# The last finish of a four-layer graph network: cosine multiply on GpSimd, statistics by tile, store in five parts

## The reference

```python
def _layernorm(x, axis=-1, eps=1e-05):
    m = jnp.mean(x, axis=axis, keepdims=True)
    v = jnp.var(x, axis=axis, keepdims=True)
    return (x - m) / jnp.sqrt(v + eps)
...
# the end of the last layer (L3)
    angle = 0.1 * (ms @ W3) * node_attr * (1.0 / np.sqrt(MUL0 + MUL1))
    cos, sin = (jnp.cos(angle), jnp.sin(angle))
    return cos * sc + sin * conv
...
x = _layernorm(x + _L0_gnn_ref(x, ...), axis=-1)
...
x = _layernorm(x + _L3_gnn_ref(x, ...), axis=-1)
```

## Time and profile before

| | us |
|---|---|
| median of three runs | 6455.58 |
| lowest, highest | 6455.34, 6458.41 |
| the profiled execution's own time | 6450.41 |
| its span | 6448.6 |
| last finish, from the sine product (6398.35) to the end of the last scaling (6439.63) | 41.28 |
| from there to the end of the span | 8.97 |

### The profile page before, as it was taken

One profiled execution on the slowest core, in us unless ns is written; L12 is line 12 of the kernel. 1 busy time (PEld: TensorE's weight loads), 2 busy tenths in 40 slices (PEclk: granted clock), 3 DMA queues, 4 the chain that ended last, 5 costly groups with the idle time before them and its releaser, 6 DMA issues. The chain is left out here.

```text
span 6448.6 us, 162454 instructions
## 1 busy us (share of the span) xinstructions
PE 4844.0 (75%) x45499; PEld 3772.4 (58%) x45500; DVE 4815.1 (75%) x10999; ACT 2313.8 (36%) x6999; POOL 4226.7 (66%) x4249
## 2 busy tenths in 40 slices
PE   6666767388888888888888769876666677777775
PEld 3444445277777777777777757644444454444444
DVE  5777776488888898888888764577777756666665
ACT  1000002266666666666666567410000020000011
POOL 5777775177767777777777347277777727777771
PEclk8888888699999999999999989888888887777777
DMA  3333332133333333333333247222222212222221
GB/s 107 92 93 92 92 92 69 42 90 94 92 89 92 89 92 92 90 92 91 90 92 89 67 148 229 62 73 73 72 72 72 72 40 70 69 69 69 69 69 35
DMA packets 401394, 545.14 MB, mean 85 GB/s; under 512 B 144934, under 2 KB 283318, under 8 KB 401180
## 3 DMA queue, kind: packets, MB, share of 16 engines
q0 software_dynamic: 193920, 331.22, 21.0%
q1 hardware_dynamic: 207388, 212.84, 11.3%
HBM read 464.79 MB, written 78.90 MB: 84 GB/s over the span
## 5 line engine op out<-in xcount | busy, mean ns | idle before, releaser
L805 POOL DMA_INDIRECT e_rows<-tab,e_idx x2424 | 2291.2, 945 | 811.0 <-issue 690.4
L1074 POOL DMA_INDIRECT acc<-tabx,a_idx x1616 | 1686.5, 1044 | 869.9 <-issue 467.9
L850 PE MATMUL e_wps<-e_w,e_hidT 64*128 64x192 f32 (+1 forms) x4848 | 790.6, 460 | 874.6 <-DVE e_hidT L921 871.5
L850 PEld LDWEIGHTS e_wps<-e_w,e_hidT 64*128 64x128 f32 x4848 | 538.2, 250 | 1079.1 <-DVE e_hidT L921 965.4
L835 PE MATMUL e_win<-e_feat,e_ohy 128*32 128x96 f32 (+1 forms) x19392 | 1025.6, 330 | 27.1 <-DVE e_feat L915 25.6
L835 PEld LDWEIGHTS e_win<-e_feat,e_ohy 128*32 128x32 f32 x19392 | 707.2, 131 | 455.9 <-issue 293.9
L906 DVE TENSOR_TENSOR e_feat<-e_wps,e_rows 128x256 f32<-128x256 f32 x606 | 257.5, 425 | 834.5 <-DMA e_rows<-tab,e_idx 761.2
L915 DVE TENSOR_TENSOR e_feat<-e_wps,e_rows 128x384 f32<-128x384 f32 (+1 forms) x1616 | 720.5, 498 | 0.0
L1137 PE MATMUL a_c<-acc,a_buffer 128*128 128x64 f32 (+1 forms) x4848 | 624.9, 272 | 121.6 <-ACT a_buffer L1115 121.6
L824 ACT ACTIVATE e_idx<-src 128x4 int32 (+1 forms) x606 | 123.2, 204 | 1606.4 <-DMA e_rows<-tab,e_idx 1585.1
L1137 PEld LDWEIGHTS a_c<-acc,a_buffer 128*128 128x128 f32 (+1 forms) x4848 | 590.5, 192 | 143.6 <-issue 143.6
(11 more groups left out here) (252 smaller groups left out, 7851.2 us busy)
## 6 DMA issues: line engine op xcount, KB each, us to landing
h_d<-a_buffer SPq DMA_DIRECT2D x202, 322.0 KB, 2.5
s_hin<-h_d SPq DMA_DIRECT2D x202, 322.0 KB, 3.5
e_rows<-tab,e_idx POOLq DMA_INDIRECT x2424
e_ein<-in_e64T SPq DMA_DIRECT2D x202, 128.0 KB
acc<-tabx,a_idx POOLq DMA_INDIRECT x1616
a_ein<-in_e_h SPq DMA_DIRECT2D x202, 64.0 KB
e_ein<-in_e16T SPq DMA_DIRECT2D x202, 32.0 KB
tab<-p_rows SPq DMA_DIRECT2D x36, 160.0 KB
```

Of the source, the lines that this page charges most:

```text
L805: pool.indirect_dma_start(out=rows[:, s, t, :], out_offset=None, in_=k.tab0, in_offset=bass.IndirectOffsetOnAxis(ap=idx[:, s, t:t + 1], ax ...
L850: mm = pe.matmul(wps[:, e, 2 * u + j, 0:WC], hidT[half, edges], w2[half, :], start=True, stop=True)
L1074: pool.indirect_dma_start(out=rows[:, b, q, :], out_offset=None, in_=table, in_offset=bass.IndirectOffsetOnAxis(ap=idx[:, b, end, q:q + 1] ...
```

## The change

- `layer_norm` has one path: it always takes statistics. Layers 0 and 3, which have none, make them inside `finish` by 25 `bn_stats`, one for each tile, with no wait between them.
- In layer 3 the product of `sc` and the cosine is GpSimd's (L580 of the new kernel). DVE signals `cos_ready` after the two answers of ACT, multiplies `out_all` by the sine, adds it to `x`, waits for GpSimd's `turned`, and adds `f_tmp` to `x`. Before, `f_tmp` was added to `out_all` first; the number of additions is the same.
- The last scaling is cut into five operations over five tiles each, with no wait between them, and SP sends each part by a DMA of its own as soon as it is scaled, and waits for all at the end.

```diff
-def layer_norm(v, act_do, link, k, x, tmp, m, stats=None, D_=D):
+def layer_norm(v, act_do, link, k, x, tmp, m, stats, scale=True, D_=D):
 
     n = x.shape[1]
-    if stats is None:
-        link(v.tensor_reduce(m[:, 0, :], x, AX.X, ALU.add))
-        link(v.tensor_scalar(m[:, 0, :], m[:, 0, :], 1.0 / D_, None, ALU.mult))
-        link(v.tensor_tensor(x, x, over(m[:, 0, :], 2, D_), ALU.subtract))
-        link(v.tensor_tensor(tmp, x, x, ALU.mult))
-        link(v.tensor_reduce(m[:, 1, :], tmp, AX.X, ALU.add))
-    else:
-        ...
+    link(v.tensor_tensor(m[:, 1, :], stats[:, :, 1], stats[:, :, 4], ALU.subtract))
+    link(v.tensor_tensor(m[:, 1, :], m[:, 1, :], m[:, 1, :], ALU.mult))
+    link(v.tensor_tensor(m[:, 2, :], stats[:, :, 2], stats[:, :, 5], ALU.add))
+    link(v.scalar_tensor_tensor(m[:, 1, :], m[:, 1, :], D_ / 4, m[:, 2, :], ALU.mult, ALU.add))
     link(v.tensor_scalar(m[:, 1, :], m[:, 1, :], 1.0 / D_, EPS, ALU.mult, ALU.add))
-    ...
+    link(v.tensor_tensor(m[:, 0, :], stats[:, :, 1], stats[:, :, 4], ALU.add))
+    link(v.tensor_scalar(m[:, 0, :], m[:, 0, :], 0.5, None, ALU.mult))
+    link(v.tensor_tensor(x, x, over(m[:, 0, :], 2, D_), ALU.subtract))
     act_do()
     inverse_root(v, link, m[:, 1, :], m[:, 2, :], m[:, 0, :])
-    link(v.tensor_tensor(x, x, over(m[:, 2, :], 2, D_), ALU.mult))
+    if scale:
+        link(v.tensor_tensor(x, x, over(m[:, 2, :], 2, D_), ALU.mult))
...
+        own = h.sb(name + "own_stats", [P, n, 6]) if stats is None else stats
+        parts = [(t, min(5, n - t)) for t in range(0, n, 5)]
...
                 if out is not None:
-                    sp.wait_ge(asked, len(jobs) + 1)
-                    sp.dma_start(out.rearrange("(t p) d -> p t d", p=P), x[:, :, :]).then_inc(stored, 16)
-                    sp.wait_ge(stored, 16)
+                    for j, (t, many) in enumerate(parts):
+                        sp.wait_ge(normed, j + 1)
+                        sp.dma_start(out.rearrange("(t p) d -> p t d", p=P)[:, t:t + many, :], x[:, t:t + many, :]).then_inc(stored, 16)
+                    sp.wait_ge(stored, 16 * len(parts))
+
+            @block.gpsimd
+            def _(pool):
+                if L == 3:
+                    pool.wait_ge(cos_ready, 1)
+                    pool.tensor_tensor(tmp[:, :, :], k.sc[:, :, 0:D], over(col[:, 4, :], 2, D), ALU.mult).then_inc(turned, 1)
...
                     ask()
                     ask()
+                    v.sem_inc(cos_ready)
                     link(v.tensor_tensor(o[:, :, 0:D], o[:, :, 0:D], over(col[:, 3, :], 2, D), ALU.mult))
-                    link(v.tensor_tensor(tmp[:, :, :], k.sc[:, :, 0:D], over(col[:, 4, :], 2, D), ALU.mult))
-                    link(v.tensor_tensor(o[:, :, 0:D], o[:, :, 0:D], tmp[:, :, :], ALU.add))
                     link(v.tensor_tensor(x[:, :, :], x[:, :, :], o[:, :, 0:D], ALU.add))
-                layer_norm(v, ask, link, k, x[:, :, :], tmp[:, :, :], m, stats)
-                v.sem_inc(asked)
+                    v.wait_ge(turned, 1)
+                    link(v.tensor_tensor(x[:, :, :], x[:, :, :], tmp[:, :, :], ALU.add))
+                if stats is None:
+                    for t in range(n):
+                        ins = v.bn_stats(own[:, t, :], x[:, t, :])
+                    link(ins)
+                layer_norm(v, ask, link, k, x[:, :, :], tmp[:, :, :], m, own, scale=out is None)
+                if out is not None:
+                    for t, many in parts:
+                        here = x[:, t:t + many, :]
+                        v.tensor_tensor(here, here, over(m[:, 2, t:t + many], 2, D), ALU.mult).then_inc(normed, 1)
```

More of the change, by code:

```diff
@@ L558, in finish @@
         asked, answered, stored = h.sem(name + "asked"), h.sem(name + "answered"), h.sem(name + "stored")
+        cos_ready, turned, normed = h.sem(name + "cos_ready"), h.sem(name + "turned"), h.sem(name + "normed")
+        own = h.sb(name + "own_stats", [P, n, 6]) if stats is None else stats
+        parts = [(t, min(5, n - t)) for t in range(0, n, 5)]
         jobs = []
```

## The result

The changed kernel took 6442.19 us in the median of 13 runs (6436.21 to 6446.46), the kernel before 6456.58 in 13 runs beside it (6451.65 to 6459.1): a ratio of 0.9977, with a 95% interval from 0.9971 to 0.9984. That is 14.4 us less; 9.4 had been forecast, and the time lies inside the range. Its profiled execution took 6445.45 us.

A forecast was written before the change was run, and what follows sets the result against it. DVE's serial work in the finishes, then the store, was taken to bound the kernel. Layer 0's 5.3 us plus layer 3's 4.1 made 9.4 us off 6455.58, giving 6446.2 us, range 6436 to 6451.

The forecast's parts named there:

- Bound: Finishes of layers 0 and 3: DVE's serial chain sets the time, so each microsecond off it leaves the kernel.
- The exclusion: Layer 3: GpSimd's product and DVE's two-SBUF-input operations run one after the other, 4.36 + 4.36 + 8.2 us plus 0.3.
- GpSimd's product: Layer 3, cosine product moved to GpSimd: 8.2 us in proportion to 512 elements, 7.5 as cheap end.
- Rival A: Layer 3: GpSimd's product runs unhindered beside DVE, 8.5 us less; gain 17.9, 6437.7 us; chance 0.25.
- rival C: Layer 3, L628 and L629: engines change hands within operations, 250 changes cost 32 us; 23 us slower, 6478 us; chance 0.04.
- the 0.3 for handing over: Layer 3: passing the turn between DVE and GpSimd was to add 0.3 us to their serial times.
- The statistics: Layers 0 and 3: 25 `bn_stats` without waits at 0.26 us each, 6.6 us in all, bounds 6.2 and 8.2.
- The small operations: Layer 3, after the `bn_stats`: seven 25-wide DVE operations of about 0.22 us each, 1.6 us together.
- The store: End of layer 3: five 400 KB DMAs end 8.97 us after the first part is ready, plus 0.3 for four more starts.
- Rival B: End of layer 3: the store's parts don't overlap, 13.8 us in a row; gain only 3.9, 6451.7 us; chance 0.07.
- the cheap end of the case: Both finishes: `bn_stats` 6.2 twice, GpSimd 7.5, no handover, nothing extra for the store; gain 11.5 us.
- its own case: Whole kernel: the main forecast, engines serialised, gain 9.4 us to 6446.2, spanning 6443 to 6451 with run spread; chance 0.64.

The follow-up runs named there:

- the run with four forms: Changed kernel plus 24 VectorE operations of 512 elements beside 100 short GpSimd ones, before layer 3's sine product: two-input forms 0.824 us each, one-input sum 0.687.
- the run in which GpSimd came second: Changed kernel with the sine product cut so GpSimd starts after its first tile: 15.34 us to the start of L632, against 15.43 in the changed kernel.
- the second: The changed kernel unaltered, timed again beside the kernel before: 6441.23 us against 6454.97, ratio 0.9978, 13.7 us less.

## Why the prediction was right, and where its sizes were off

- Bound: right. Only the two finishes changed, and each microsecond by which VectorE's chain there became shorter left the kernel.
- The exclusion, on which the forecast turned: right; of the two readings, for it and the earlier trace rows against it, the prediction took the first. Its reason was thin: L909 too is a product with broadcast operands, so only the length set L1226 apart, and the run with four forms showed that L909's form excludes GpSimd's product as well. Counting would have helped more: in the trace of before 396 gathers of L1074 start during an L1226, and the 317 of them that took over 1.1 us all end 0.81 to 0.83 us after it, so the earlier trace rows is the rule there and not a chance row. The Trainium skill's rule (SBUF — State Buffer, Who interferes with whom) agrees with the trace in each point that was run: two SBUF inputs exclude GpSimd, one does not (5.76 us), and the lock holds for the whole operation (11.04 = 6.87 + 4.17). Rival A, side by side, falls; rival C, changing hands within operations, falls by the run in which GpSimd came second: two changes of hand in all.
- Which of the orders it would be was left open, and the runs showed that both give the same, 15.4 and 15.3 us.
- GpSimd's product: mis-sized. 8.2 us was taken in proportion to 512 elements, with 7.5 as the cheap end; it took 6.87, or 1.72 ns an element. The short ones of 160 elements take 0.452, so an element costs 1.67 ns and the fixed part is 0.18 us, not 0.1 as estimated from the memset; even that gives only 1.04 for 512, which is the 1047 ns of the earlier trace rows. The row was right and the split of it was wrong. With the 0.3 for handing over, which cost nothing, that is 1.6 us too much.
- The statistics: mis-sized in the same direction. 6.6 us was taken for 25, with 6.2 as the cheap end; they took 5.79 to the next operation, twice. They start 0.23 us apart, not 0.26: without a wait each is recorded with 0.308 instead of 0.327 and overlaps the next by 0.08. That is 1.6 us in the two layers.
- The small operations (1.58 us for seven, 1.6 forecast), the subtraction and the root (1.70) were as worked out. The store: 9.11 us after the first part was ready, 9.27 forecast. Rival B, parts that don't overlap, falls: with one DMA the stretch is 3.46 us longer. The rule for large DMAs (the Trainium skill, DMA: Bandwidth & Descriptors, Bandwidth) did not bite here, where the DMAs stand queued behind each other: 305 to 319 GB/s with 400 KB each.
- So the sum was 13.0 instead of 9.4 us, past the cheap end of the case, 11.5, since both unknown durations came out below their bounds. The experiments split it: statistics 6.1 and 6.1, the store in parts 3.5, and GpSimd's product -2.5; together 13.2.
- What was luck: the time, 6442.19, lies in the range of 6436 to 6451, but just outside what the prediction gave its own case, 6443 to 6451. The room below had been left for rival A, which did not come true. And the gain of 14.4 us is past the 12.9 that the prediction took for the least that can be told from no change (its interval is 10.3 to 18.7 us); that outcome had a chance of 0.34 in all, and 0.09 by the way it came about, cheap `bn_stats` and a cheap product.
- The remaining 1.4 us of the first measurement (14.4), and 0.7 of the second, lie within the intervals.

## What to carry to other kernels

Before moving VectorE work to GpSimd, count the SBUF inputs of what VectorE does meanwhile: beside operations with two, GpSimd's time is added and not hidden, and the move loses what GpSimd is slower by; beside operations with one it was free, and so it was beside operations with their other operand in PSUM, the memory that TensorE writes: in the kernel before, the 202 products of L1593 took 1038 to 1052 ns each, whether or not L1685, which reads PSUM, was at work beside them, and L1685's operations kept 372 to 389. ScalarE hid the same product fully. Look for busy times longer than the same shape takes elsewhere: here a wait for the other engine is recorded as work. And at the end of a kernel, statistics by tile (6.1 us) and a store cut into parts (3.5 us) were each worth about as much as a pass of VectorE over the data (4.36 us).

## What the runs showed that was not expected

- A waiting GpSimd operation gets in between two VectorE operations only 0.04 us apart, and a waiting VectorE operation gets in between GpSimd's short ones: with both queues full they take strict turns, 0.86 us for a pair in the run with four forms, where VectorE's operations are recorded with 0.824 us and GpSimd's, which take 0.452 alone, with 0.895.
- Why the gathers of L805 were never held up beside L909 (574 start during it and take 0.956 us at most) while those of L1074 were beside L1226 stays open. It is not the form of L909, which does exclude a GpSimd product. What differs between the two gathers was not tried.
- At 160 elements and with no wait between them, VectorE's operations with a number for each partition as an operand started 0.30 us (fused product and addition) and 0.27 us apart (subtraction and scaling), the statistics 0.23. The operations differ in kind too, so that the number is what costs is not shown.
- The same kernel took 6455 us at a granted clock of 0.885 and 9254 to 9499 at 0.68, with GpSimd's, VectorE's and the store's durations in the last finish unchanged. Over the whole span TensorE's busy time was 4844 us before and 6740 with the product back on VectorE, VectorE's 4815 and 4827.
